# Edge counts with two target columns packed into one, 128-wide one-hot weights, and two accumulators used in turn; the first weight product right behind them

## The reference

```
src, dst = edge_index
e   = leaky_relu(al_s[src] + al_d[dst], 0.2)
m   = segment_max(e, dst);   ex = exp(e - m[dst])
z   = segment_sum(ex, dst);  alpha = ex / (z[dst] + 1e-16)
out = segment_sum(h[src] * alpha, dst)                    # GAT, both layers
...
seg = edge_type * n + dst
cnt = segment_sum(ones, seg)                              # per relation and target
mean = segment_sum(x[src], seg) / maximum(cnt, 1.0)
deg = segment_sum(ones, dst) + 1.0
```

## Time and profile before

| | value |
|---|---|
| median of 3 runs | 1584.8 us |
| profiled execution, span | 1601.9 us |
| PE, DVE, ACT, POOL busy | 90%, 59%, 33%, 38% |
| chain that ended last, by engine | PE 80%, DVE 10%, DMA 4% |
| chain, by line | relation products L2364 25%, counting L2086 8% |
| counting, PE | from 5.85 to 148.57 us |
| ranks, W1 tiles and `al`, to the first head | from 148.57 to 216.05 us |

### The profile page before, as it was taken

The page is one execution under the profiler, slowest core; times in us unless marked ns, Lnnn a source line. Parts: engine busy times, 40 slices in busy tenths (PEclk is TensorE's granted clock), DMA queues, the critical chain, the costliest instruction groups (busy, mean ns, idle before and its releaser), DMA issues.

```text
span 1601.9 us, 23265 instructions
## 1 busy us (share of the span) xinstructions
PE 1447.0 (90%) x7904; PEld 1154.4 (72%) x7904; DVE 937.6 (59%) x2170; ACT 536.5 (33%) x622; POOL 613.6 (38%) x520
## 2 busy tenths in 40 slices
PE   8999966787999998899999999999679989989991
PEld 7887656764565554899999999999647655556660
DVE  6644678866624735466556666656348751366654
ACT  0001036532211102455554555555236541123330
POOL 0000077777766651434434343333158730111102
PEclk9999878879979998899999999999889989989996
DMA  7101900002017121688788787787669860426635
GB/s 193 36 0 4 124 2 2 2 1 60 2 18 224 39 61 64 250 275 279 274 286 290 268 273 273 281 285 278 180 207 321 273 187 18 122 65 210 203 110 166
DMA packets 114255, 248.50 MB, mean 155 GB/s; under 512 B 30461, under 2 KB 52154, under 8 KB 114092
## 3 DMA queue, kind: packets, MB, share of 16 engines
q1 hardware_dynamic: 79228, 141.18, 29.3%
q0 software_dynamic: 22432, 72.27, 15.7%
q10 hardware_dynamic: 12528, 34.22, 5.5%
HBM read 206.77 MB, written 45.31 MB: 157 GB/s over the span
## 4 chain that ended last, share of the span: by engine, by line
PE 80%; DVE 10%; DMA 4%; issue 3%; ACT 2%; POOL 0%; DVEq 0%; ACTq 0%; SPq 0%; POOLq 0%; another core or an unknown queue 0%; PEldq 0%
PE PS L2364 25%; PE PS L2086 8%; PE PS L2282 5%; PE PS L2321 5%; PE PS L2545 4%; PE PS L2474 4%; PE PS L2556 3%; PE PS L2354 3%; PE PS L2459 3%; PE PS L2146 3%; PE PS L2223 3%; PE PS L2512 2%; PE PS L2251 2%; PE PS L2493 2%; DVE e L1155 2%
## 5 line engine op out<-in xcount | busy, mean ns | idle before, releaser
L709 POOL DMA_INDIRECT xg<-xn_dram,xrow x70 | 117.7, 1681 | 321.0 <-DVEq L1333 266.4
L2364 PE MATMUL PS<-whi,xhi 128*128 128x384 f32 x840 | 222.3, 345 | 8.7 <-DVEq L1706 8.7
L2364 PE MATMUL PS<-whi,xlo 128*128 128x384 f32 x840 | 215.7, 338 | 0.0
L2364 PE MATMUL PS<-wlo,xhi 128*128 128x384 f32 x840 | 214.3, 336 | 0.0
L1155 DVE TENSOR_TENSOR wlo<-raw,whi 128x2304 fp32r<-128x2304 f32 x72 | 185.6, 2577 | 44.6 <-ACTq L946 37.3
L944 ACT ACTIVATE whi<-raw 128x2304 fp32r<-128x2304 f32 x72 | 153.6, 2133 | 18.8 <-DMA raw<-in_L_gnn_W_rel 8.5
L2364 PEld LDWEIGHTS PS<-whi,xhi 128*128 128x128 f32 x840 | 149.5, 190 | 9.1 <-DVEq L1706 9.1
L2364 PEld LDWEIGHTS PS<-wlo,xhi 128*128 128x128 f32 x840 | 153.2, 189 | 0.0
L2364 PEld LDWEIGHTS PS<-whi,xlo 128*128 128x128 f32 x840 | 152.6, 189 | 0.0
L1155 DVE TENSOR_TENSOR xlo<-PS,xhi 128x768 fp32r<-128x768 f32 x70 | 67.0, 958 | 145.3 <-ACTq L955 140.4
L2086 PE MATMUL PS<-hot_dr,hot_s 125*125 125x512 bf16 (+9 forms) x880 | 134.7, 301 | 5.9 <-DVE hot_dr L1212 5.9
(11 more groups left out here) (384 smaller groups left out, 2536.0 us busy)
## 6 DMA issues: line engine op xcount, KB each, us to landing
raw<-in_L_gnn_W_rel SPq DMA_DIRECT2D x72, 1152.0 KB
z_dram<-xn ACTq DMA_DIRECT2D x70, 384.0 KB, 7.5
wroot<-in_L_ffn_w SPq DMA_DIRECT2D x12, 576.0 KB, 6.1
y_dram<-yb ACTq DMA_DIRECT2D x17, 384.0 KB, 4.0
pre<-in_L_ffn_w SPq DMA_DIRECT2D x9, 576.0 KB, 5.5
gw<-in_L_gnn_W SPq DMA_DIRECT2D x2, 2304.0 KB, 27.2
fw<-in_L_ffn_w SPq DMA_DIRECT2D x8, 576.0 KB
fw<-in_L_ffn_w SPq DMA_DIRECT2D x1, 4608.0 KB
```

What stands on the lines that cost most here:

```text
L709: pool.indirect_dma_start(xg[b][j][:, :], None, xn_dram, bass.IndirectOffsetOnAxis(ap=xrow[:, b, j:j + 1], axis=0)).then_inc(x_gathered[b] ...
L2364: mm = pe.matmul(slot(q)[:, s * BANK:s * BANK + HALF], a[:, k, :], wt[:, k, s * HALF:(s + 1) * HALF], start=(k == 0 and part == 0), stop=( ...
```

## The change

Counting: the target index d is split into d mod 313 (`PAIR`) and a high part; the one-hot of d mod 313 holds 1 for a low target and 4096 (`PACK`) for a high one, so one fp32 sum carries two counts. A source tile then streams 34 + 313 = 347 columns where it streamed 659. The one-hots are laid out in tiles of 128, so every weight is 128 wide; the counts by relation and target come from one matmul, of 128 weight columns that begin with the relation, and 313 columns, with relations on the partitions. The sum over all chunks needs 4 banks; three rounds of 24, 32 and 24 chunks go to the lower, the upper and the lower half of PSUM, so that each fp32 sum stays exact and can be unpacked while the other half is filled: ACT takes out the high part, DVE the low part, and they are added up over the rounds. The relation one-hots of four chunks are written by one instruction.

Order: DVE waits for `ld_x` after 12 chunks; the transposes of x go between the last 12 chunks; W1's first tile follows the last chunk; the ranks and five small transposes (which bring the relation counts to target partitions) come behind that tile, the ranks of rows behind the second; on DVE `inv` comes after the unpacking, the second half of the grouping before the `al` of tile 1, and `eplace` before the `al` of tile 4.

```
@@
+PAIR = -(-N // 2)
+PACK = 4096
+UNPACK_BIAS = -0.488
+PK = REL + PAIR
+HOT_REL = T * 128
+REGION = 2048
+ROUND = [0, 24, 56, ET]
+FOUR = 4
@@ scalar
+            def unpack_high(n):
+                act.wait_ge(onehots_used, ROUND[n + 1])
+                step(act.activation(limb[n][:, :, :], packed(n)[:, :, REL:PK], ACT.Copy, bias=UNPACK_BIAS, scale=1.0 / PACK))
+                step.do(act.activation(rel_high[n][:, :], packed_relations(n), ACT.Copy, bias=UNPACK_BIAS, scale=1.0 / PACK))
+                act.sem_inc(high_ready, 1)
@@ vector
-                if not first:
-                    dve.wait_ge(onehots_used, j + b - AHEAD + 1)
-                dve.tensor_scalar(hot_s[b][:, :], iota16[:, 0:N], ef[:, 0, bass.ds(j + b, 1)], None, ALU.is_equal)
-                dve.tensor_scalar(hot_dr[b][:, 0:N], iota16[:, 0:N], ef[:, 1, bass.ds(j + b, 1)], None, ALU.is_equal)
-                dve.tensor_scalar(hot_dr[b][:, N:N + REL], iota34[:, :], ef[:, 2, bass.ds(j + b, 1)], None,
-                                  ALU.is_equal).then_inc(onehots_ready, 1)
+                b = j % AHEAD
+                if b % FOUR == 0:
+                    if j >= AHEAD:
+                        dve.wait_ge(onehots_used, j + FOUR - AHEAD)
+                    tt(onehot[:, b:b + FOUR, HOT_REL:HOT_DST], iota34[:, :].unsqueeze(1).broadcast_to([EP, FOUR, REL]),
+                       ef[:, 2, j:j + FOUR].unsqueeze(2).broadcast_to([EP, FOUR, REL]), ALU.is_equal)
+                dve.tensor_scalar(onehot[:, b, 0:HOT_REL], iota_tiles[0:EP, :], ef[:, 0, j:j + 1], None, ALU.is_equal)
+                dve.tensor_scalar(onehot[:, b, HOT_DST:HOT_DST + PAIR], iota16[:, 0:PAIR], dst_pair[:, 0, j:j + 1], dst_pair[:, 1, j:j + 1],
+                                  ALU.is_equal, ALU.mult).then_inc(onehots_ready, 1)
+            def unpack_steps(n):
+                v, rv = packed(n), packed_relations(n)
+                lows, relations = counts[:, :, 0:PAIR], counts[:, :, N:N + REL]
+                dve.wait_ge(high_ready, n + 1)
+                step(dve.scalar_tensor_tensor(lows if n == 0 else low_part, limb[n][:, :, :], float(-PACK), v[:, :, REL:PK], ALU.mult, ALU.add))
+                yield
+                step(dve.scalar_tensor_tensor(relc[:, 0:PAIR] if n == 0 else rel_part, rel_high[n][:, :], float(-PACK), rv, ALU.mult, ALU.add))
...
+            for j in range(12):
+                onehots(j)
             dve.wait_ge(ld_x, 16)
             do(dve.memset(xn_all[96:128, :, :], 0.0))
+            for j in range(12, ET):
+                onehots(j)
+                if j % 2 and j < 64:
                     next(first_norm, None)
+                if j in range(ROUND[1] + AHEAD + 4, ROUND[1] + AHEAD + 12, 2):
+                    next(unpack0, None)
+                if j in range(ROUND[2] + AHEAD + 2, ET, 2):
+                    next(unpack1, None)
...
             for t in range(T):
+                if t == 1:
+                    for _ in grouping:
+                        pass
+                    dve.sem_inc(tables_ready, 1)
+                if t == 4:
+                    edge_places()
                 dve.wait_ge(h_ready, t + 1)
@@ tensor
+            def count(b, n, start):
+                first = n % 2 * REGION
                 for i in range(T):
+                    for o, c, m in piece(0, first + i * PK, PK):
+                        pe.matmul(PS[:, c:c + m], onehot[:, b, i * 128:(i + 1) * 128], onehot[:, b, HOT_REL + o:HOT_REL + o + m],
                                   start=start and c % BANK == 0, stop=False, skip_group_check=True)
+                return pe.matmul(PS[:, first + T * PK:first + REGION], onehot[:, b, HOT_REL:HOT_REL + 128], onehot[:, b, HOT_DST:HOT_DST + PAIR],
+                                 start=False, stop=False, skip_group_check=True)
...
+            for j in range(ROUND[2], ET):
+                count_chunk(j, 2)
+                k = j - (ET - 2 * K)
+                if k == 0:
+                    pe.wait_ge(region_free, 2)
+                    pe.wait_ge(xn_ready, T)
+                if k >= 0 and k % 2 == 0:
+                    k //= 2
+                    take("turn1", 2 + k % 2, k // 2)
                     for t in range(T):
+                        mm = pe.transpose(psT(2 + k % 2)[:, t, 0:P], xn[:, t, k * 128:(k + 1) * 128], ident[0:P, 0:P])
+                    mm.then_inc(full[2 + k % 2], 1)
...
             for t, (q, n) in enumerate(W1_SLOT):
...
+                if t == 0:
+                    source_ranks()
+                    relations_of_targets()
+                if t == 1:
+                    rows_before()
```

More of the change, by code:

```diff
@@ L2119, in spread @@
                 mm.then_inc(full[q], 1)
-            turn("turn1", xn, lambda: pe.wait_ge(xn_ready, T))
-            pe.wait_ge(cnt_ready, 2)
-            pe.wait_ge(tables_ready, PRES_TABLE)
-            pe.wait_ge(consts_ready, 2)
-            take("ranks", 1, 0)
-            for i in range(T):
-                for t in range(i + 1):
-                    pe.matmul(slot(1)[0:P, i * REL:(i + 1) * REL], before[:, :] if t == i else ones[0:P, 0:P], pres[:, t, :],
-                              start=(t == 0), stop=(t == i))
@@ new lines, in source_ranks @@
+            def source_ranks():
+                pe.wait_ge(tables_ready, PRES_TABLE)
+                take("ranks", 1, 0)
+                for i in range(T):
+                    for t in range(i + 1):
+                        pe.matmul(slot(1)[0:P, i * REL:(i + 1) * REL], before[:, :] if t == i else ones[0:P, 0:P], pres[:, t, :],
+                                  start=(t == 0), stop=(t == i))
+                for t in range(T):
+                    mm = pe.matmul(slot(1)[0:P, BANK:BANK + REL], ones[0:P, 0:P], pres[:, t, :], start=(t == 0), stop=(t == T - 1))
+                mm.then_inc(full[1], 1)
@@ L2140, in _, with rows_before @@
+            def rows_before():
+                pe.wait_ge(tables_ready, IN_ROW_TABLE)
+                take("ranks", 0, 0)
+                pe.matmul(slot(0)[0:P, 0:T], before[:, :], in_row[:, :], start=True, stop=True)
+                pe.matmul(slot(0)[0:P, BANK:BANK + T], ones[0:P, 0:P], in_row[:, :], start=True, stop=True).then_inc(full[0], 1)
+            pe.wait_ge(consts_ready, 2)
             pe.wait_ge(ld_w1, 16)
```

238 lines of the change are left out of this document (132 added, 106 removed).

## The result

| | before | after |
|---|---|---|
| median of 4 runs each, same chip | 1584.64 us | 1547.57 us (1541.95 to 1552.19) |
| ratio, 95% interval | | 0.9753 (0.9721 to 0.9785) |
| profiled execution, span | 1601.9 us | 1546.0 us |

37 us faster by the medians, 34 to 44 by the interval of the ratio; forecast were 44.6. The profiled spans differ by 56 us. Most of that difference beyond 37 lies in stages that the change doesn't touch; experiments 1, 5 and 12 go into it.

What follows compares the result with a forecast made beforehand. PE's streamed columns were taken to bound counting. Counting ending 49.5 us earlier, less a 4.9 us longer tail, gives 44.6 us gained: 1584.8 - 44.6 = 1540 us, with an 8-in-10 range of 1526 to 1551.

Steps and rivals of the forecast that it cites:

- likeliest case: Whole kernel: the forecast as worked out, 1540 us, own range 1533 to 1548; chance 62%.
- One sign that the prediction named against itself: Counting: the prediction is wrong if PE waits for one-hots between chunks 12 and 80.
- PE's chunk: Counting on PE: nine matmuls, 2048 columns, 0.89 us a chunk instead of 1.754, between 0.85 and 1.03.
- DVE's chunk: Counting on DVE: writing a chunk's one-hots takes 0.57 us, up to 0.81, under PE's 0.89.
- The wait for x: Counting: x lands at about 28.1 us, so PE idles 13 us, from 19 to 32.2; lower clock costs 2.4 more.
- The end of counting: PE's last count comes at 99 us, 49.5 earlier than 148.57.
- The tail: Last chunk to last `al`, before the heads: 71.9 us where it was 67.0, 4.9 longer, give or take 3.
- Downstream: After the first head: PE comes 44.6 us earlier, POOL 37; 7.4 of 14 us room used, no new wait.
- rival 2: Counting: DVE becomes the bound, with the 313-wide instruction at 0.45 us; 1547 us, chance 15%.
- Rival 3: Counting: the wait for x is shorter or misread, so the 13 us pause and clock loss go; 1525 us, 12%.
- rival 4: Tables: `inv` and `in_row` come 7 us later, `fw2` lands after PE asks; 1552 us or so, 8%.
- rival 5: Counting: DVE's one-hots run at 1.1 ns a column throughout, 1.35 us a chunk; 1582 us, chance 3%.

Runs made afterwards that it cites:

- experiment 1: The kernel before, unchanged, profiled a second time: span 1592.6 us, messages stage 131.4 us; its set's median was 1594.6 us.
- experiment 5: The changed kernel, unchanged, run again on another chip: 1544.6 us, ratio 0.9740 to the kernel before.
- experiment 12: The kernel before, unchanged, profiled a third time: messages stage 132.7 us; its set's median was 1595.7 us.
- experiment 11: The changed kernel with each counting chunk's last product (313 columns) issued twice: ratio 0.9806 to the kernel before.
- experiment 4: The changed kernel with the counting's stationary one-hots 125 instead of 128 columns wide: ratio 0.9756 to the kernel before.
- experiment 6: The changed kernel with the load of x cut at partition 120 into two transfers: 1534.0 us, ratio 0.9665 to the kernel before.
- experiment 2: The changed kernel with W1's load issued only once x has landed: ratio 0.9702 to the kernel before.
- experiment 3: The changed kernel with DVE's wait for x behind 20 chunks of one-hots instead of 12: ratio 0.9731 to the kernel before.
- experiment 7: The changed kernel with the whole grouping and its signal ahead of the third unpacking on DVE: 1542.7 us, ratio 0.9727 to the kernel before.
- experiment 8: The changed kernel with the edge places ahead of the attention terms of tile 2 instead of tile 4: 1546.9 us, ratio 0.9738 to the kernel before.

## Why the prediction was right, point by point

The time, 1547.6 us, lies in the range (1526 to 1551) and, just, in the likeliest case's own (1533 to 1548). The mechanism was right, several sizes were not. One sign that the prediction named against itself came true: PE did wait for one-hots between chunks 12 and 80. It is a size, not another mechanism, for the sum has 0.7 us for it.

- **PE's chunk.** 0.89 forecast, 0.90 measured; columns set the pace (experiment 11). The bound of 1.03 without the quick weight load was far too high: 0.93 (experiment 4), that is 9 ns a product over the columns. In the kernel before, more than half of the surplus of 0.32 us lies with the five products of 34 columns, which take 0.25 us for 0.07 us of columns:

```profile
29.05 0.41 PE L2090 MATMUL PS<-hot_dr 125*125 125x34 bf16 x5
29.30 1.66 PE L2086 MATMUL PS<-hot_dr,hot_s 125*125 125x512 bf16 x11
```

Whether weights of 128 would have sped these up no run shows. The sentence that 9.5 us hang on the 128 weights is refuted for the changed kernel; it is 2 to 3 us.
- **DVE's chunk.** 0.57 forecast. The pair takes 0.57 instead of 0.51, so a chunk is 0.62: the 313-wide one-hot with two operands per partition costs 0.27, not 0.21, and not the bound of 0.45. DVE starved PE between 57 and 66 us, for 2.0 us instead of 0.7: eight chunks take 9.2 us (56.97 to 66.14) where 7.2 are their pace. In experiment 6, where PE isn't late, the same costs 3.4 us.
- **The wait for x.** Forecast 19 to 32.2 us, measured 20.8 to 32.28 (PE began at 7.0 instead of 5.9, which costs nothing here); memset forecast 28.1, measured 28.05; clock loss forecast 2.4, measured 2.2. Experiments 2, 3 and 6 show the cause. The step "the transfer doesn't move" held; that it needn't be so slow was not seen.
- **The end of counting.** 99 forecast, 101.0 measured: 1.3 us of starving more and 0.7 of pace (68 x 0.01).
- **The tail.** `PRES_TABLE` 9.4 forecast, 9.2 measured; PE's wait 1.6, measured 1.1. The step that failed is the next: "I take 5.3 with part of it slow, and 0.6 for the small transposes" was 8.25 us (110.27 to 118.52), at a clock of 0.61. PE came from a busy tile and paused for 1.1 us only, yet the granted clock was 0.61 over the ranks. Over the profiles of this kernel and its variants the ranks with the small transposes took 6.1 to 9.2 us, so part of this miss is the execution. From there all stands 2 to 3 us late: `INV_TABLE` 19.5 for 17.5, `in_row` 36.0 for 33.7, PE's wait for it 8.8 for 9.5, the last tile 65.8 for 62.9, the last `al` 74.6 for 71.9. The form of the tail, with `eplace` right before the last `al`, is as forecast.
- **Downstream.** No new wait at `fw2`, as said. The room was less than worked out, since the first thing to be late is not `fw2` but the small tables that SP carries behind it: gone once PE came 4 to 8 us earlier and SP's load of `fw2` did not (experiments 2, 7 and 8). The time of the gathers, 304 to 314 us, was taken as fixed.
- **The sum.** 40.1 us at the first head instead of 44.6, the two steps above: 2 from counting and 2.7 from the tail. From 1584.8 this makes 1544.7; the other 2.9 us lie within the interval. The profiled execution was forecast at 1557 us and took 1546.0: the 17 us between span and median of the kernel before were its own execution and did not carry over. Both errors of the sum point the same way; that the time still fell inside the likeliest case's bounds, by 0.4 us, is partly luck.

Of the rivals, 2 (1547, DVE as the bound) hit the time, but not by its mechanism: DVE's chunk is 0.62 us, not 0.81. Rival 3 fell with experiments 2 and 6, which show what the pause costs; 4 became true only in the experiments that went further, and its 1552 is mis-added: 37 less 7 leaves a gain of 30, or 1555. Nothing of 5 showed.

## What to carry to other kernels

A shorter stage runs into what stood beside it: ask at what time each input lands, not only how long the work takes, and count the engines that a load can use (125 partitions used a third of them; cutting the load at 120 gave a quarter as much again as the whole change). A wait that is removed late in a stage is worth only what the slowest side chain allows: compare the shift of every chain (here POOL's gathers behind `zrow`), not only that of the busiest engine. And take more than one profile, of both kernels and in more than one set of runs: first head to `wroot` differed by 6 us between profiles of the kernel before, while its messages took 131 to 133 us each time, and only the variants of the changed kernel showed that this stage can take 118 or 136 us. A gain read from one profile, such as that of experiment 6 at the first head, can hold 2 us that belong to the execution, and adding such gains up carries them along.
